# 64-wide attention heads in a four-layer kernel: masks and scores two slots ahead moved to stand in front of the products with the values

## The reference, cut to what matters

```python
def _L3_xattn_ref(q, k, v, Wq, bq, Wk, bk, Wv, bv, Wo, bo):
    B, S, D = (2, 256, 128)
    H, HD = (16, 64)
    b, s, _ = q.shape
    qh = (q @ Wq.T + bq).reshape(b, s, H, HD).transpose(0, 2, 1, 3)
    kh = (k @ Wk.T + bk).reshape(b, s, H, HD).transpose(0, 2, 1, 3)
    vh = (v @ Wv.T + bv).reshape(b, s, H, HD).transpose(0, 2, 1, 3)
    scores = jnp.einsum('bhqd,bhkd->bhqk', qh, kh) / np.sqrt(HD).astype(np.float32)
    causal = jnp.tril(jnp.ones((s, s), bool))
    scores = jnp.where(causal, scores, -jnp.inf)
    attn = jax.nn.softmax(scores, axis=-1)
    out = jnp.einsum('bhqk,bhkd->bhqd', attn, vh)
    out = out.transpose(0, 2, 1, 3).reshape(b, s, H * HD)
    return out @ Wo.T + bo
...
x = x + _L3_xattn_ref(_layernorm(x, axis=-1), ctx_1024, ctx_1024, L3_xattn_Wq, ...)
```

## Time and profile before

| | us |
|---|---|
| median of three runs | 2555.81 |
| lowest and highest run | 2552.15 and 2559.61 |
| the profiled execution's own time | 2550.41 |
| its span, first to last instruction | 2548.6 |
| TensorE busy | 2162.0 (85%) |
| VectorE, ScalarE, GpSimd busy | 1245.9, 921.4, 512.5 |
| mean granted TensorE clock | 0.92 of full speed |
| `wide_heads`, first scores to last output | 1924 to 2375 |

### The profile page before, as it was taken

How to read it: one execution, slowest core, us unless ns; L and a number is a source line. 1 busy time by engine, 2 the same in 40 slices (tenths; PEclk the granted TensorE clock), 3 DMA queues, 4 the chain that set the end, 5 groups by cost and what they waited for, 6 DMA issues and landing times. The chain is left out here.

```text
span 2548.6 us, 50126 instructions
## 1 busy us (share of the span) xinstructions
PE 2162.0 (85%) x19952; PEld 1437.5 (56%) x19952; DVE 1245.9 (49%) x3260; ACT 921.4 (36%) x2319; POOL 512.5 (20%) x478
## 2 busy tenths in 40 slices
PE   3999854875599999799969999999989999999555
PEld 1555543763487788355535555555555666667521
DVE  4566545663412121566644444444435555555476
ACT  1333211663244443233323333323215556656200
POOL 4222003663111110222210011100102333333100
PEclk8999956786699999899979999999989999999698
DMA  4000000000000000200000000000010000000001
GB/s 135 11 11 7 2 0 24 14 5 5 0 2 2 2 1 2 84 11 11 3 2 1 1 0 0 0 0 1 1 43 5 5 6 10 5 1 2 1 0 33
DMA packets 21012, 28.33 MB, mean 11 GB/s; under 512 B 4302, under 2 KB 15574, under 8 KB 20310
## 3 DMA queue, kind: packets, MB, share of 16 engines
q1 hardware_dynamic: 20808, 25.40, 3.2%
HBM read 23.30 MB, written 2.10 MB: 10 GB/s over the span
## 5 line engine op out<-in xcount | busy, mean ns | idle before, releaser
L1722 ACT ACTIVATE arena<-quad,arena 114x512 f32<-114x512 f32 x192 | 131.2, 687 | 350.7 <-PE quad L1678 350.6
L1807 DVE SCALAR_TENSOR_TENSOR arena<-quad,arena 114x512 f32<-114x512 f32 x192 | 142.9, 750 | 219.2 <-ACT arena L1722 218.2
L529 DVE TENSOR_REDUCE arena<-pair 128x8 f32<-128x1024 f32 x128 | 156.8, 1225 | 155.1 <-PE pair L360 152.6
L1677 PE MATMUL quad<-arena,wide 128*114 128x512 f32 x384 | 204.3, 614 | 21.0 <-DVE arena L1807 21.0
L236 POOL TENSOR_TENSOR rstd<-var_eps,neg_half 128x4 f32<-128x4 f32 (+1 forms) x64 | 66.1, 1033 | 674.2 <-DVE var_eps L232 580.2
L1678 PE MATMUL quad<-arena,wide 128*114 128x512 f32 x384 | 196.9, 594 | 0.0
L1666 PEld LDWEIGHTS single<-wide,arena 114*128 114x128 f32 x1536 | 180.4, 192 | 27.5 <-issue 27.5
L2222 POOL TENSOR_TENSOR arena<-arena 128x512 f32<-128x512 f32 x128 | 130.5, 1041 | 312.2 <-DVE arena L2145 312.2
L1666 PE MATMUL single<-wide,arena 114*128 114x128 f32 x1536 | 180.6, 275 | 0.0
L611 POOL TENSOR_SCALAR arena<-arena 128x512 f32<-128x512 f32 x56 | 86.8, 1569 | 331.2 <-ACT arena L465 331.2
L1458 ACT ACTIVATE arena<-quad,arena 128x256 f32<-128x256 f32 x256 | 111.1, 476 | 108.5 <-PE quad L1387 108.4
(11 more groups left out here) (400 smaller groups left out, 4221.6 us busy)
## 6 DMA issues: line engine op xcount, KB each, us to landing
arena<-in_ctxT SPq DMA_DIRECT2D x32, 256.0 KB, 2.7
wide<-in_w SPq DMA_DIRECT2D x2, 2048.0 KB, 10.7
wide<-in_wgu SPq DMA_DIRECT2D x1, 2736.0 KB
x<-in_x SPq DMA_DIRECT2D x4, 512.0 KB, 6.0
out_x<-x SPq DMA_DIRECT2D x8, 256.0 KB, 3.6
wide<-in_w SPq DMA_DIRECT2D x1, 1368.0 KB
we<-in_we SPq DMA_DIRECT2D x1, 512.0 KB, 12.2
wide<-in_wq SPq DMA_DIRECT2D x1, 512.0 KB, 3.3
```

The source lines that it names most:

```text
L529: dve.tensor_reduce(mx[m % 2][:, 8 * p:8 * p + 8], S[:].rearrange("p (h k) -> p h k", h=8), AX.X, ALU.max).then_inc(s["s_free"], 1)
L1677: pe.matmul(bank[2 + k % 2][0:FR, :], wg[:, e, cols], xnT[u], start=True, stop=True)
L1722: act.activation(sg[0:FR, k % 2, :], bank[2 + k % 2][0:FR, :], ACT.Silu, bias=bgc[0:FR, e, f:f + 1]).then_inc(s["sg_ready"], 1)
L1807: dve.scalar_tensor_tensor(out=hid[e % 2][0:FR, f, :], in0=bank[4 + k % 2][0:FR, :], scalar=b1c[0:FR, e, f:f + 1], in1=sg[0:FR, k % 2, :], ...
```

## The change

Nothing is computed differently and no tile is added. Three statements move inside the loops over t8. On TensorE `scores(t8 + 2)` goes from the start of the slot, ahead of the transposes, to behind the early projections, in front of `attend(t8 - 1)`. On ScalarE the early `keep` comes first, and `copy_o(t8 - 1)` now stands between the two halves of the exponentials. On VectorE `maximum(t8 + 2)` goes from behind `invert(t8 + 1)` to behind the two copies of transposed probabilities and the early `keep`. `ring_order` is unchanged, since the scores don't use the ring.

```diff
--- before.py
+++ after.py
@@ -2041,12 +2041,12 @@
                     project(n, 0, c)
                 turn(1)
                 for t8 in range(N8):
-                    if t8 + 2 < N8:
-                        scores(t8 + 2)
                     turn_probs(t8)
                     early, late = slot_pieces(t8)
                     for piece in early:
                         project(*piece)
+                    if t8 + 2 < N8:
+                        scores(t8 + 2)
                     if t8 >= 1:
                         attend(t8 - 1)
                     if t8 % 2 and t8 >= 3:
@@ -2102,14 +2102,14 @@
                 turned(1)
                 for t8 in range(N8):
                     early, late = slot_pieces(t8)
-                    if t8 + 2 < N8:
-                        exps(t8 + 2, 0)
                     for piece in early[0:1]:
                         keep(*piece)
                     if t8 + 2 < N8:
-                        exps(t8 + 2, 1)
+                        exps(t8 + 2, 0)
                     if t8 >= 1:
                         copy_o(t8 - 1)
+                    if t8 + 2 < N8:
+                        exps(t8 + 2, 1)
                     for piece in late[0:1]:
                         keep(*piece)
                     if t8 % 8 == 7 and t8 // 8 + 2 < NG:
@@ -2192,12 +2192,12 @@
                     early, late = slot_pieces(t8)
                     if t8 + 1 < N8:
                         invert(t8 + 1)
-                    if t8 + 2 < N8:
-                        maximum(t8 + 2)
                     copy_pt(t8, 0)
                     copy_pt(t8, 1)
                     for piece in early[1:2]:
                         keep(*piece)
+                    if t8 + 2 < N8:
+                        maximum(t8 + 2)
                     if t8 % 8 == 4 and t8 // 8 + 2 < NG:
                         normed(t8 // 8 + 2)
                     if t8 % 8 == 2 and t8 >= 8:
```

## The result

The changed kernel takes 2621.73 us (median of four runs, 2621.03 to 2624.69) against 2555.10 for the kernel before (four runs too, 2552.15 to 2559.61). The ratio is 1.0262, with a 95% interval of 1.0246 to 1.0279: 63 to 71 us slower. The forecast was 2612 with a range of 2583 to 2638: the result lies inside, 10 us above the forecast.

The account below looks back on a forecast made before the run. The prediction took TensorE's own work as the bound. Added standing of 42 + 5.3 + 7.3 + 5.5 + 0 = 60 us on the profiled 2550.4 gave 2610.5; it forecast 2612 us, range 2583 to 2638.

Parts of the forecast that it names:

- TensorE sets the pace before, so an order can save only seams: Slots with projections: TensorE is busy for all of 389 us, so reordering saves at most seams between kinds of matmul.
- The circle of the even slots: Next odd slot's first piece waits for ScalarE's late copy: 8.64 us against 7.11, 42 us over 28 slots.
- The transposed x: Odd slots where the next group's first q product waits for x's copy: 8.50 against 7.61, six times, 5.3 us.
- The last group: VectorE and ScalarE wait on each other there: 5.9 to 6.0 us a slot against 4.47, 7.3 us in all.
- The start: Phase's first scores fall behind transposes and early pieces, 3.9 us later; 1.6 more in following slots, 5.5 in all.
- Seams at nothing: Changed neighbours among TensorE's matmuls: 0 us in sum, with 6 us either way put into the range.
- the row from 1350 to 1875 us: Earlier stretch of the trace: clock 1.00 at 495 of 525 us busy, read as no clock loss from short standing.
- the second rival: TensorE falls to 1.2 GHz in part of the phase: 40 us more over 28 pairs, 2652 us; chance 13%.
- a clock off 1.00: Sign against the forecast: TensorE's granted clock in the changed phase leaving 1.00.
- The last rival's turning point: No slower, or faster (5%): the bank is free 4.96 us after scores, not 6.49, needing exponentials 0.19 us apart, not 0.34.

Follow-up runs that it names:

- the third order: Kernel before, with scores behind the transposes and ahead of the early pieces, except in the first two and last eight slots: 2558.11 us against 2556.05, ratio 1.0008.
- one copy more: Changed kernel, with ScalarE reading the late piece's bank once more into a spare tile ahead of the real copy: 2653.17 us, ratio 1.0395 to the kernel before.
- three copies more: Changed kernel, with ScalarE reading the late piece's bank three times more into spare tiles ahead of the real copy: 2728.37 us, ratio 1.0689 to the kernel before.

## Why the prediction was right

- *TensorE sets the pace before, so an order can save only seams.* Held: every order that made no wait (ScalarE alone, the third order) is within 0.2% of the kernel before.
- *The circle of the even slots.* Held link by link. It was 0.10 us short, 8.74 instead of 8.64: when TensorE starts again after the wait, the first piece takes 0.96 to the second, where the earlier trace rows has 0.86 for a piece right behind the transposes in a running stream. With v the step is 8.65, because its copy takes 0.65 and not q's 0.73, and the prediction took them as the same. Over 28 steps the term was 45 instead of 42.
- *The transposed x.* Held, with the copy of x as releaser; 8.71 instead of 8.50. The copy of x starts 5.70 us after the scores, just as summed (2333.86 - 2328.16); the 0.21 come behind it: 0.05 from a longer copy, 0.09 until TensorE starts, 0.07 in the restarted pieces.
- *The last group.* The circle held, 5.94 for 5.9 to 6.0, and the experiment with the old order there confirms it. That the whole came to 8.3 for 7.3 is partly luck: the steps from scores 58 on gave 6.3, the two pieces that changed their place took 1.9 off, and the last stretch gave 3.8, part of it through a clock the prediction had at full.
- *The start.* Held: the first moved scores come 16.31 - 10.96 = 5.3 us later instead of 3.9, the rest in the next steps; 6 in sum for 5.5.
- *Seams at nothing.* The odd slots gained 0.15 us each, 3 us in all, within the bound given.
- *The clock.* At 1.31 us of standing in every other slot it stayed at 1.00, so the row from 1350 to 1875 us was the right neighbour and the second rival did not come true in the slots with projections. The prediction named a clock off 1.00 as a sign of being wrong, and at the end of the last group it did fall, to 0.50 from 2433.3 to 2440 us. It was close in the slots too: one copy more in the same place brought it about. By the rule on shortly interrupted matmul streams in the Trainium skill, TensorE: Matmul & The Clock Gate (A second HAM failure mode: psum-queue depth-cycling), the changed kernel would have been hit throughout; from 1951 to 2395 us it was not, at a clock of 1.00, while the kernels with one and three copies more, at 0.95 and 0.86, behave as the rule says.
- *The last rival's turning point.* It says that the exponentials would have to be 0.19 us apart instead of 0.34. The sum gives 0.15: the row would have to be 6.49 - 4.96 = 1.53 us shorter over eight, which is 0.19 less for each. Nothing else hangs on it.
- *Where the forecast was low.* Of the 9.7 us, 3.1 lie in the starting point: the forecast was built on 2552 (2612 less 60), and the median of before is 2555.1. Then the phase grew by 62.6 and not 60. The measured difference is 66.6 us; the remaining 4 are inside the scatter of the phases ahead, and no run here tells them apart from it.

## What to carry to other kernels

When work is moved within a software pipeline, write down for each ring buffer the time from the moved instruction to the release of the buffer, and from the moved instruction to the next wish for it; the change is free as long as the first is smaller, and costs the difference once a turn when it is not, as long as the clock stays full. A reordering on the engine that is the bound needs the others' orders moved with it: alone, TensorE's part cost 167 us and VectorE's 104, together with ScalarE's they cost 67. And look at the copy that stands last behind a long row on its engine; moved up by four exponentials it gave back 42 of the 67.

## What the runs showed of the hardware that I had not expected

The price of standing is not even. TensorE idle for 9% to 13% of the stretch from 2100 to 2340 us, in waits of no more than 1.4 us, kept its full clock (changed kernel 217.46 of 240 us busy; `copy_o` last, in waits of 1.37 and 0.87 us, 208.67 of 240, also 1.00). With waits of 1.8 and 1.9 us (one copy more), at about the same share, 210.67 of 240, it fell in ten of 28 even steps, to 0.95 over the stretch. Waits of 2.0 us went with 0.96 where they came in every other slot (VectorE's part alone, 204.60 of 240) and with 0.89 where they came in every slot (TensorE's part alone, 193.14 of 240), waits of 3 us (three copies more, 200.58 of 240) with 0.86. With one copy more the even steps at the lower clock grew by another 0.9 to 1.7 us, most of them by 1.6, so that 0.57 us of added waiting in a slot cost 31 us over the kernel instead of 16.

And a seam between two kinds of matmul has no fixed price. The transposes took 0.93 us before a piece in the kernel before, 0.88 in the changed one and 0.96 before masks. A piece took 0.86 to the next piece right behind transposes (2296.69 to 2297.55, kernel before), 0.96 behind transposes after a wait, and 0.96 also without a wait behind the product with the values (2299.53 to 2300.49, kernel before).
